# One core's transformer sandwich: batch 0's norm behind the MLP is spread over later units

## The reference

```
x = x + ln(attention(ln(x)))      # 32 heads of 8, 8 key/value heads, causal, sign-quantized weights
x = x + ln(ffn(ln(x)))            # silu(x@W1.T) * (x@W3.T), 1024 hidden, Hadamard transform, @W2.T
x = x + ln(mix(ln(x)))            # token shift mixes, keys, values, receptances, a scan over tokens, Wo
x = x + ln(moe(ln(x)))            # 32 experts of 96, top 4, and a shared expert of 704
```

## Time and profile before

| | us |
|---|---|
| timed runs | 526.77, 526.46, 522.57 (median 526.46) |
| profiled execution | 521.88 |
| its span | 519.9 |

### The profile page before, as it was taken

How to read it: one execution, slowest core, us unless ns; L and a number is a source line. 1 busy time by engine, 2 the same in 40 slices (tenths; PEclk the granted TensorE clock), 3 DMA queues, 4 the chain that set the end, 5 groups by cost and what they waited for, 6 DMA issues and landing times.

```text
span 519.9 us, 10001 instructions
## 1 busy us (share of the span) xinstructions
PE 432.7 (83%) x3396; PEld 297.6 (57%) x3396; DVE 341.6 (66%) x851; ACT 280.8 (54%) x554; POOL 235.9 (45%) x316
## 2 busy tenths in 40 slices
PE   7987899899998799787987347698889899999654
PEld 2664455454555387676775325487668566666343
DVE  5976687688782758546469956995743555555346
ACT  7645767677776631424855188434432455555302
POOL 7874553456674305102402371337465155555600
PEclk9978999899999999898999667789989999999968
DMA  8345345111110298000000101899622454444182
GB/s 231 112 128 157 79 133 143 37 39 48 31 28 4 84 315 265 1 1 0 1 1 0 31 0 32 230 226 298 204 89 91 101 151 134 135 129 126 53 326 84
DMA packets 51674, 55.63 MB, mean 107 GB/s; under 512 B 10080, under 2 KB 42729, under 8 KB 51624
## 3 DMA queue, kind: packets, MB, share of 16 engines
q1 hardware_dynamic: 47176, 46.26, 32.5%
q0 software_dynamic: 4448, 8.73, 4.9%
HBM read 35.22 MB, written 21.73 MB: 110 GB/s over the span
## 4 chain that ended last, share of the span: by engine, by line
PE 47%; DVE 25%; issue 8%; SPq 7%; ACT 6%; DMA 4%; POOL 2%; POOLq 0%; DVEq 0%; ACTq 0%
PE ps L2470 7%; PE ps L2186 5%; PE ps L2236 5%; PE ps L2165 4%; PE ps L2224 4%; PE ps L2495 4%; PE ps L2226 4%; PE ps L2225 3%; PE ps L2451 3%; DVE st L1032 3%; PE ps L2144 3%; SPq L564 2%; DVE h_lo L1200 2%; SPq L592 2%; DMA max_parts_scratch<-m_cols 2%
## 5 line engine op out<-in xcount | busy, mean ns | idle before, releaser
L1765 ACT ACTIVATE probs<-ps 128x512 f32<-128x512 f32 x160 | 87.0, 598 | 34.7 <-PE ps L2165 33.4
L1133 DVE TENSOR_REDUCE negm<-ps 128x2 f32<-128x1024 f32 (+1 forms) x64 | 67.4, 1081 | 14.6 <-PE ps L2154 14.5
L897 POOL DMA_INDIRECT y_slots_scratch<-yblk,ids x48 | 47.2, 984 | 47.9 <-issue 30.9
L712 POOL TENSOR_TENSOR rstd<-ve,halfneg 128x4 f32<-128x4 f32 x15 | 15.8, 1053 | 82.8 <-DVE ve L1051 27.5
L2186 PE MATMUL ps<-probs,v_all 128*32 128x128 f32 (+3 forms) x512 | 48.3, 452 | 2.1 <-DVE att L1161 1.6
L1801 ACT CAST h_hi<-hf 128x512 fp32r<-128x512 f32 x28 | 17.4, 620 | 60.4 <-DVE hf L1191 60.4
L2165 PE MATMUL ps<-q_ring,k_all 64*128 64x512 f32 (+3 forms) x256 | 40.2, 371 | 11.0 <-DMA q_ring<-max_parts_scratch 5.3
L2144 PE MATMUL ps<-k_all,q_ring 64*128 64x512 f32 (+3 forms) x256 | 46.5, 374 | 2.5 <-DVE negm L1133 1.4
L2165 PEld LDWEIGHTS ps<-q_ring,k_all 64*128 64x128 f32 x256 | 20.8, 186 | 44.4 <-ACT probs L1765 32.0
L1528 DVE COPY xcol<-ps 128x256 f32<-128x256 f32 x48 | 20.4, 424 | 34.9 <-PE ps L2451 34.9
L2470 PE MATMUL ps<-wgu,xcol 128*64 x188 | 40.6, 339 | 0.0
(11 more groups left out here) (367 smaller groups left out, 1349.4 us busy)
## 6 DMA issues: line engine op xcount, KB each, us to landing
x_sorted_scratch<-pad SPq DMA_DIRECT2D x6, 1072.0 KB, 13.0
xblk<-x_sorted_scratch SPq DMA_DIRECT2D x96, 67.0 KB
wgu<-in_moe_w SPq DMA_DIRECT2D x4, 1536.0 KB, 17.8
ycomb<-y_slots_scratch SPq DMA_DIRECT2D x8, 512.0 KB, 6.7
q_ring<-q_parts_scratch SPq DMA_DIRECT2D x60, 64.0 KB
wd<-in_moe_w SPq DMA_DIRECT2D x1, 3072.0 KB, 21.1
sraw<-in_moe_w SPq DMA_DIRECT2D x6, 384.0 KB, 3.3
q_parts_scratch<-qparts SPq DMA_DIRECT2D x4, 512.0 KB, 4.8
```

Source lines behind the costliest of these rows:

```text
L897: pool.indirect_dma_start(out=y_slots, out_offset=bass.IndirectOffsetOnAxis(ap=ids[:, i:i + 1], axis=0), in_=yblk[:, i % YR, :], in_offset ...
L1133: dve.tensor_reduce(negm[:, par, :, hp, qt], pair_of, AX.X, ALU.max, negate=True).then_inc(s1_read, 1)
L1765: act.activation(probs[:, par, u, :], ps[:, col_unit(g, u), :], ACT.Exp)\
```

## The change

On DVE, `out_stats(1, 0)` moves from behind unit 7 to behind unit 8, `out_apply(1, 0)` from behind unit 8 to behind unit 9, `in_apply(1, 0)` from behind unit 8 to behind unit 10, and the three mixes from behind units 9, 10, 11 to behind units 11, 12, 13. `first_keys` stays behind unit 12, now after the second mix. On ACT, the columns and the three mixes move from units 9, 10, 11 to 11, 12, 13, and `shift(1, 0)` with the third mix from 11 to 13; `first_exponents` stays at unit 12, now behind the second mix. On PE, the transposes move from between up(10) and down(9) to between up(11) and down(10). POOL and SP are unchanged.

```diff
--- before.py
+++ after.py
@@ -1301,13 +1301,14 @@
                     in_apply(0, 1)
                 if u == 5:
                     split_low(1, 1)
-                if u == HC - 1:
+                if u == HC:
                     out_stats(1, 0)
-                if u == HC:
+                if u == HC + 1:
                     out_apply(1, 0)
+                if u == HC + 2:
                     in_apply(1, 0)
-                if 9 <= u < 12:
-                    mixes(0, u - 9)
+                if 11 <= u < 14:
+                    mixes(0, u - 11)
                 if u == 12:
                     first_keys()
 
@@ -1894,16 +1895,15 @@
                 if u == 5:
                     split_high(1, 1)
                     shift(0, 1)
-                if u == 9:
+                if u == 11:
                     columns(0)
                     mixes(0, 0)
-                if u == 10:
+                if u == 12:
                     mixes(0, 1)
-                if u == 11:
+                    first_exponents()
+                if u == 13:
                     mixes(0, 2)
                     shift(1, 0)
-                if u == 12:
-                    first_exponents()
             for u in range(B * HC - 2, B * HC):
                 act.wait_ge(mul_done, u - 1)
                 silu(u, 2 * (u % 2), u % 2)
```

## The result

| | median us | runs | ratio to before |
|---|---|---|---|
| before | 526.62 | 522.57 to 530.08 | |
| changed | 519.86 | 518.00 to 522.41 | 0.9897 (0.9855 to 0.9938) |
| changed, run again | 520.41 | 514.98 to 521.40 | 0.9867 (0.9784 to 0.9950) |

What follows compares the result with a forecast made beforehand. PE was taken to bound each MLP unit (4.20 us), stalled by DVE's lumped norm; gate(14) would come 4.0 or 2.4 us earlier, middle 3.2, and 525.3 less 3.2 gave 522.1 us, range 517.9 to 527.0.

Steps and rivals of the forecast that it cites:

- PE bound per unit, DVE's lumps the cause: MLP's second half: PE bounds each 4.20 us unit; batch 0's norm in two lumps on DVE stalls PE 1.47 and 2.94 us.
- Spread over units 8, 9, 10: DVE: statistics, residual and rows behind successive units; the 1.47 us stall goes, PE waits 2.1 us at the transposes, not 2.94.
- The clock at the transposes: PE: transposes and the down behind them at full clock or as slow as before (4.30 us), making gate(12) 0 or 1.66 us later.
- ACT's chain sets gate(14): From columns at 242.69 to silu(14) at 263.85 ACT is the late engine; PE would be done by 261.5.
- Sum: Gate(14) moves from 268.45 to 264.45 or 266.1: a gain of 4.0 or 2.4 us, middle taken as 3.2.
- The total: Whole kernel: mean of the known executions before, 525.3 us, less 3.2 gives 522.1 us.
- Table switch by the page's rule: ACT's two table switches: the skill's drain of about 1.38 us each would cost 2.8 us more, leaving a gain of 0.4.
- Late last downs: Rival, PE at the receptances: idling about 4.6 us brings half clock, downs up to 2.7 us late, 524.8 us; chance 0.12.
- Slower by a clock that stays low: Rival, PE from the transposes on: clock stays at 1.2 GHz, gate(14) 11 us later than before, 536.6 us; chance 0.05.
- DVE beside POOL: DVE's h_lo(12) starts at the very end of POOL's low parts: cost 0 to 0.94 us, taken as 0.

Runs made afterwards that it cites:

- both edits: From the changed kernel, block constants moved behind unit 6 and ScalarE's shift of xa behind the silu of unit 15: 520.34 us (0.9897), once more 518.08 us (0.9873).

## Why the prediction was right, point by point

- **PE bound per unit, DVE's lumps the cause.** Right. The experiment with the statistics put back gives 1.5 us for that wait; undoing the spreading altogether costs 7.2 us once the transposes are late (48.29 against 41.11).
- **Spread over units 8, 9, 10.** The gates were worked out at 4.20, 9.22, 15.04 and 18.57 us after gate(7); they came at 4.20, 9.14, 14.84 and 18.31. The stall of 2.1 us ahead of the transposes is 1.76.
- **The clock at the transposes.** This was the term I could not size: 0 or 1.66 us, and I took half. The low clock did not come behind the wait of 1.76 us, and the whole 1.66 was there. My middle was a hedge between two cases, and which of them came was luck. That the length of the wait decides it is not shown (see the last section). Shown by the clock of 1.00 from 246 to 250 and by the transposes' 1.10 us.
- **ACT's chain sets gate(14).** Right: 20.95 us from columns to silu(14), where I had 21.2, and moving the shift out of it moved gate(14) by 1.6 us. It is not ACT's work alone: 2.1 of the 20.95 us are waits for DVE.
- **Sum.** 4.46 us against 4.0 (full clock) and 3.2 (my middle). Of the 0.5 us beyond 4.0, 0.26 came on DVE ahead of the columns (gate(11) at 18.31 instead of 18.57) and 0.2 on ACT's chain. The distances held small waits: the exponentials took 2.39 us back to back (257.32 to 259.71), where I had 2.64.
- **The total.** Predicted 522.1, measured 519.86 and 520.41. The middle part gives 1.3 us of the difference. My base works the other way: it was the lower of the two averages of before (525.3 against a median of 526.5), and from the higher one I would have said 523.3. By the medians the kernel gained 6.8 and 5.1 us, more than the 4.5 of the part that was edited; the first part, which moves by 2 to 4 us between traces of the same code, could cover that. That the total lies inside a range of 9 us, which held nearly no gain too, says little by itself. What bears the prediction out is the middle part.
- **Table switch by the page's rule.** ScalarE's silu starts at 261.01, right behind the load at 259.71 with 1.28 us, and its exponentials at 257.32 behind the load at 256.02. The drain that the Trainium skill adds (ScalarE: Activation LUTs, What ACT_TABLE_LOAD costs) does not appear at either switch; the measurement decides.
- **Late last downs.** The low clock did come behind the 4.11 us wait: the last down ended at 282.0 against batch 1's statistics at 283.60, so the slack shrank from 3.2 to 1.6 us and covered it. So the rival's mechanism was there, and of the size that was priced for a short low spell: receptances and last downs took 7.5 us instead of 5.9. It is not what came out with the shift moved: there the wait ahead of the receptances shrank to 2.51 us, and the low clock at `mix_out` lies behind another wait.
- **Slower by a clock that stays low.** Did not happen here. With the transposes put back the clock did fall behind the wait of 5.96 us, but it was back after about 4 us (1.00 from 247 us).
- **DVE beside POOL.** The product took 1.65 us again at the same place, and the `h_lo` of unit 12 took 0.69: no cost.

## What to carry to other kernels

When a helper engine's late work stalls the busy one, two things must move together: spread the helper's work over the holes of several units, and move its consumer on the busy engine late enough that the busy engine has other work until then. Either alone lost here (with the columns and mixes late in both cases). Before trusting a total, cut the span at events that the change cannot pass: the part that was edited measured to 0.1 us while the totals of one kernel scattered by over 1%. And when the edited part gains and the total does not, look behind it, at the clock behind the next waits and at waits for DMAs, before going on to shorten the same chain.

## What the runs showed of the hardware

- TensorE's clock after a wait: waits of 1.02, 1.48, 1.54 and 1.76 us were followed by full clock, 2.94, 4.90 and 5.96 us by 1.2 GHz at once or within half a microsecond. After the 4.11 us ahead of the receptances it fell about a microsecond into them. But the wait alone does not decide: with both edits, in identical code, the receptances began at half clock behind 2.52 us in one trace and at full clock behind 2.53 us in the other, and in the changed kernel the clock also fell 2 us behind a wait of only 0.70 us (at about 285.7 us, in `mix_out`). The two rows:

```profile
273.44 0.80 PE L2225 MATMUL ps<-m_hi,rwhi 128*128 128x512 f32 x1 [2.52 <-DVE num L1233]
```

```profile
269.43 0.50 PE L2225 MATMUL ps<-m_hi,rwhi 128*128 128x512 f32 x1 [2.53 <-DVE num L1233]
```

- Work that only keeps TensorE busy moved the low stretches instead of removing them (granted clock 0.83 for 0.71 behind gate(14), 0.91 for 0.97 in the shared units), and the changed kernel's ratio to before went from 0.9897 and 0.9867 to 0.9952 (the intervals still overlap).
- Code ahead of the change took 222.4 to 229.2 us in the 13 traces, and 225.2 and 229.2 in two traces of identical code, with waits for the small copies of row maxima through DRAM among it (2.10 us at one of them in the changed trace, 1.43 in the one before). Whether these explain all of it I did not test.
